# Local attention: VectorE's sum of squares moved ahead of its score maxima

## The reference, cut to what matters

```python
qkv = x @ Wqkv; q, k, v = jnp.split(qkv, 3, -1)
q = l2norm(q) * qs;  k = l2norm(k) * ksc       # t / max(norm(t), 1e-12), per head of 64
q = q * cos * scale + rotate_half(q) * sin * scale
k = k * cos * inv   + rotate_half(k) * sin * inv
sim = einsum(q, k) * 8.0, masked to a window of 32 back
out = softmax(sim) @ v
return out.reshape(b, n, INNER) @ Wo
```

## Time and profile before

| what | us |
|---|---|
| median of three runs | 5260.53 |
| the profiled execution | 5253.03 |
| its span, first to last instruction | 5251.2 |
| TensorE busy | 4463.1 (85%) |
| VectorE busy | 3855.7 (73%) |
| ScalarE busy | 3330.9 (63%) |
| GpSimd busy | 2830.8 (54%) |
| mean granted clock of TensorE | 0.929 of full |

### The profile page before, as it was taken

How to read it: one execution, slowest core, us unless ns; L and a number is a source line. 1 busy time by engine, 2 the same in 40 slices (tenths; PEclk the granted TensorE clock), 3 DMA queues, 4 the chain that set the end, 5 groups by cost and what they waited for, 6 DMA issues and landing times. The chain is left out here.

```text
span 5251.2 us, 198115 instructions
## 1 busy us (share of the span) xinstructions
PE 4463.1 (85%) x70278; PEld 2798.3 (53%) x70372; DVE 3855.7 (73%) x8097; ACT 3330.9 (63%) x11394; POOL 2830.8 (54%) x2108
## 2 busy tenths in 40 slices
PE   5999999698897988979889656988979889798896
PEld 1333332266565665656656534665656656566565
DVE  7888787486785867858768545867858678587784
ACT  1777777575675766747658413756747668476673
POOL 3000000476675766757667404756757667576673
PEclk6999999898998989989999877989989899898997
DMA  0000000233322323232232302323233223322333
GB/s 13 1 2 1 2 1 1 85 77 83 79 76 79 80 80 78 76 86 73 78 80 76 82 16 89 80 79 76 76 82 80 80 76 80 81 77 78 81 80 91
DMA packets 415346, 340.20 MB, mean 65 GB/s; under 512 B 170606, under 2 KB 312468, under 8 KB 412692
## 3 DMA queue, kind: packets, MB, share of 16 engines
q1 hardware_dynamic: 413972, 332.35, 23.9%
q10 hardware_dynamic: 768, 0.02, 0.0%
HBM read 100.42 MB, written 30.41 MB: 25 GB/s over the span
## 5 line engine op out<-in xcount | busy, mean ns | idle before, releaser
L936 POOL TENSOR_TENSOR f_rn<-f_ss,f_minus_half 128x8 f32<-128x8 f32 x384 | 728.4, 1897 | 397.5 <-DVE f_ss L1102 393.1
L936 POOL TENSOR_TENSOR g_rn<-g_ss,g_minus_half 128x8 f32<-128x8 f32 x384 | 728.7, 1898 | 386.3 <-DVE g_ss L1102 381.9
L427 DVE TENSOR_REDUCE a_maxima<-a_max 128x1 f32<-128x512 f32 x1024 | 651.6, 685 | 149.4 <-PE a_max L541 112.2
L351 ACT ACTIVATE a_pex<-a_scores 128x512 f32<-128x512 f32 x1024 | 531.7, 607 | 162.4 <-PE a_scores L550 161.5
L995 ACT ACTIVATE f_ex<-f_bank,f_nmx 128x64 f32<-128x64 f32 x1536 | 461.2, 314 | 135.8 <-DVE f_nmx L1095 135.3
L995 ACT ACTIVATE g_ex<-g_bank,g_nmx 128x64 f32<-128x64 f32 x1536 | 461.2, 314 | 134.4 <-DVE g_nmx L1095 133.5
L1176 PE MATMUL f_bank<-f_wqkv,f_xT 128*128 128x512 f32 x768 | 442.7, 659 | 92.7 <-DVE f_qh L1089 55.6
L1176 PE MATMUL g_bank<-g_wqkv,g_xT 128*128 128x512 f32 x768 | 442.0, 658 | 91.6 <-DVE g_qh L1089 53.6
L941 POOL TENSOR_TENSOR g_qr<-g_t 128x512 f32<-128x512 f32 x384 | 493.5, 1285 | 8.7 <-DVE g_t L1075 8.7
L941 POOL TENSOR_TENSOR f_qr<-f_t 128x512 f32<-128x512 f32 x384 | 492.2, 1282 | 8.0 <-DVE f_t L1075 8.0
L282 POOL COPY a_v_head<-a_v_all 128x128 f32 (+1 forms) x16 | 4.6, 290 | 697.3 <-PE a_sums L559 697.3
(11 more groups left out here) (236 smaller groups left out, 11153.0 us busy)
## 6 DMA issues: line engine op xcount, KB each, us to landing
f_vw<-f_vt SPq DMA_DIRECT2D x576, 128.0 KB
g_vw<-g_vt SPq DMA_DIRECT2D x576, 128.0 KB
f_vw<-f_vt SPq DMA_DIRECT2D x384, 64.0 KB
g_vw<-g_vt SPq DMA_DIRECT2D x384, 64.0 KB
f_wqkv<-in_f_Wqkv_dram SPq DMA_DIRECT2D x7, 1536.0 KB, 8.0
g_wqkv<-in_f_Wqkv_dram SPq DMA_DIRECT2D x7, 1536.0 KB, 8.5
f_xs<-xf SPq DMA_DIRECT2D x196, 32.0 KB, 1.8
g_xs<-xf SPq DMA_DIRECT2D x196, 32.0 KB, 1.8
```

Source lines behind the costliest of these rows:

```text
L351: act.activation(pex[:, kt % 2, i % NG, :], ps_s[i % 3][:], ACT.Exp).then_inc(act_ex, 1)
L427: dve.tensor_reduce(maxima[:, m // 4, m % 4:m % 4 + 1], ps_max[m % 3][:], AX.X, ALU.max).then_inc(dv_max, 1)
L936: pool.tensor_tensor(rn[:, b, :], ss[:, b, :], minus_half[:], ALU.pow).then_inc(pl_rn, 1)
```

## The change

VectorE's sum of squares and its two waits (for ScalarE's squares, and for GpSimd's root two chunks back) now stand directly behind the normalisation, ahead of the maxima of the scores and their two waits. Nothing is added or left out, and the other four engines' lists are the same.

```diff
                         dve.scalar_tensor_tensor(out=heads(qh[:, 1 - b, :]), ...).then_inc(dv_qh, 1)
+                    if real(t, c, 0):
+
+                        dve.wait_ge(act_sq, upto(act_sq, L, n))
+                        dve.wait_ge(pl_rn, upto(pl_rn, L, n - 2))
+                        dve.tensor_reduce(ss[:, b, :], heads(sq[:, b, :]), AX.X, ALU.add).then_inc(dv_ssq, 1)
                     if real(t, c, 4):
 
                         dve.wait_ge(pe_s, upto(pe_s, L, n - 4))
...
                                           negate=True).then_inc(dv_max, 1)
-                    if real(t, c, 0):
-
-                        dve.wait_ge(act_sq, upto(act_sq, L, n))
-                        dve.wait_ge(pl_rn, upto(pl_rn, L, n - 2))
-                        dve.tensor_reduce(ss[:, b, :], heads(sq[:, b, :]), AX.X, ALU.add).then_inc(dv_ssq, 1)
```

## The result

The changed kernel took 5517.51 us (median of four runs, 5509.16 to 5523.11), against 5261.29 (four runs, 5259.74 to 5274.57) for the kernel before on the same chip: ratio 1.048, 95% interval 1.0458 to 1.0502. The forecast was 5535, its own range 5440 to 5600. The profiled execution of the changed kernel took 5509.16 us, its span 5507.4; before 5253.03 and 5251.2. The mean granted clock is 0.930, before 0.929, so the clock is no part of it.

What follows compares the result with a forecast made beforehand. Two rings of 3.88 us a round, the root's and the scores', bound the kernel. Held quotients add 23.2 a layer, 278 us in twelve: 5253.03 becomes 5531, median 7.5 higher, 5538; forecast 5535 us, range 5440 to 5600.

Steps and rivals of the forecast that it cites:

- Order of starts decides: GpSimd's root against VectorE's t1: root starts at 0.25, t1 at 0.34, so the root ends at 1.90.
- the bound of 5364: If t1 wins close races at c = 2, rounds average 4.2: +103 us, 5364; chance 0.12.
- The addition comes just ahead of the quotients: GpSimd's addition at 1.87, VectorE's quotients at 1.99, held until 3.42; +0.65 us in a round of c = 2.
- c = 0 keeps 3.88 in the loop: Root starts a hair behind t1, is held until 2.52, quotients stay free, and the scores set 3.88 us.
- The rival of all rounds slow: Rounds all take 4.53 to 4.63, or TensorE's clock falls: 5638 us or more; chance 0.14.
- The held root does not hold t1 to its end: VectorE's t1 runs its 0.69 through a root of 1.65 us that started first.
- the last rival: GpSimd's root holds t1 to its end: 5.9 us a round, some 1400 us more, 6600; chance 0.02.
- By engine order alone the move is harmless: On VectorE the root's ring is cut by 0.34, the scores keep the pace at 3.88; gain next to nothing.
- the scores' ring: Maxima, exponentials, transposed probabilities' copy, weighting of values, score products, next maxima: 3.88 us a round, without the sums of squares.
- the 2 us left over for DMAs behind v: The v copy's waits for DMAs, mostly covered by longer rounds; 2 us a layer were left.
- the turn of the loop: At c = 3, t1 comes a further 0.2 late at a loop turn: 4.78 us instead of 4.57.
- all with two inputs in SBUF: VectorE's t1, t2 and quotients, having two SBUF inputs, and GpSimd's instructions shut each other out.

Runs made afterwards that it cites:

- The guard: The changed kernel, with GpSimd's addition also waiting for VectorE's quotients of the same round: 5253.65 us, ratio 0.9987.
- the cheap root: GpSimd's power replaced by an addition of the same 128x8 operands: on the kernel before 5499.05 us, on the changed kernel 5508.72 us.
- the held copy: The changed kernel with the quotients' multiplication replaced by a plain copy of the exponentials: 5452.73 us, ratio 1.0378.
- the probabilities copied first: ScalarE's transposed-probabilities copy put ahead of its q or k copy, GpSimd's addition held behind the quotients: kernel before 5232.65 us, changed kernel 5206.2 us.

## Why the prediction was right, step by step

The line of the cosine products (t1) in the changed kernel, to be laid beside the earlier trace rows:

```profile
L1073 DVE TENSOR_TENSOR f_t<-f_qh,f_rope x384: 672/676/694, 1000.3 to 3053.6; 128x512 f32<-128x512 f32 x192
```

- **Order of starts decides; the moved sums let the root start ahead of t1.** Right: root at 0.26, t1 at 0.33, root 1.65 instead of 1.93. The margin of 0.09 that had no row (the bound of 5364) went the root's way: in the first stack's rounds of c = 2 it was 0.07 to 0.08.
- **The addition comes just ahead of the quotients, which are held.** Right: 1.87 and 1.98, end at 3.42, all within 0.01 of the forecast. The guard (5254 us) and the cheap root (5499 us) show it as cause, from both sides.
- **c = 0 keeps 3.88 in the loop.** Right: 3.86 to 3.87, root 2.15. The rival of all rounds slow (5638) fell with it. But t1 was only 0.02 to 0.04 ahead of the root there; the rows gave no more than 0.01 to 0.02 for it, so that this came out as forecast is in part luck.
- **The held root does not hold t1 to its end.** Right: t1 took at most 694 ns, so the 6600 of the last rival fell. The Trainium skill, page "SBUF — State Buffer", section "SBUF: two separate sides", has the port pair held for the whole instruction. The trace agrees for the 128 x 512 addition, behind whose end the quotients end by 0.28, and not for the 128 x 8 root. What the root does differently within its 1.65 us no run tells.
- **By engine order alone the move is harmless or a small gain.** Right: 5253.65 with the guard alone, not to be told from before. It is worth 0.5%, which the prediction didn't look for, once the scores' ring is shorter.
- **Sizes.** The layer of the earlier trace rows came to 264.7 for 60 rounds, forecast 268.6. Of the 3.9: the 2 us left over for DMAs behind v were not to be seen in the length of the rounds (ScalarE's wait for them in the first stack fell from 94.5 us to 25.4); written-out tiles had 4.54 in most rounds, as forecast, except one round at 3.87 and the last at 3.95, 1.3 together; the turn of the loop cost 0.07 where I had put 0.2, for which no row stood, and there were four of them and not five, some 0.7 over a layer. From the first to the last cosine product the two stacks grew by 121.7 and 134.4 us, 21.3 a layer against 23.2 forecast. The quotients' mean was 1233 ns, where 1100 had been named: 51 of 64 were held in a middle layer, and 51 at 1.44 with 13 at 0.42 give 1.23; the 1100 was too low by my own table of rounds. So was a sign: qr was to start 0.07 to 0.2 behind t2's end, where my sum gave 0.24 (1.87 and 1.63) and 0.26 was measured. And qr that follows t2 directly starts at 1.70 by the earlier trace rows, not at 1.73, so such a round takes 4.36, not 4.39, as both kernels with the cheap root show.
- **The step that was wrong in its wording:** "all with two inputs in SBUF". True of the three instructions, but not the mark of what is shut out, as the held copy shows. The forecast didn't rest on it, since every instruction that its sum has held is one with two.

## What to carry to other kernels

Where VectorE and GpSimd work side by side, look up, before an order is changed, which of two instructions that run side by side starts first, for a wait that is taken away may be what kept them apart; a held instruction stands in the profile as a longer one, not as idle time, so compare the mean duration of a line with its shortest. Fix the order with a wait on the instruction that must go first (here the addition behind the quotients), not through timing and not by making either engine's work shorter. Then ask again what the change is worth: here -0.5% (with the probabilities copied first in both kernels) and not +4.8%.

## What the runs showed of the hardware that I had not expected

- A plain f32 copy of 128 x 256 from SBUF to SBUF is shut out by GpSimd's addition (1.31 us against 0.29), a maximum over one element of the same data is not (at most 422 ns in all 384 of each stack), so that the slower form is the faster one beside a busy GpSimd: 5254.52 against 5452.73 us.
- The race is decided by very little: quotients that started 0.01 behind the addition (1407.68 and 1407.67) were held 1.54, those 0.04 ahead of it not at all.
- Even a root without a power, 0.20 us by itself, is stretched to 0.70 if t1 has started before it.
